# The row maxima of four attention heads: one pair of VectorE reductions instead of two

## What is computed

```
q = rms_norm(linear(layernorm(x), q_w, q_b), norm_q_w)      # 8 x 112 x 512
k_img, k = rms_norm(linear(ctx[:, :257], ...)), rms_norm(linear(ctx[:, 257:], ...))
img_x = softmax(q k_img^T / sqrt(32)) v_img                 # 16 heads
txt_x = softmax(q k^T / sqrt(32)) v
x = x + linear(img_x + txt_x, o_w, o_b)
x = x + sum over the top 2 of 8 experts: weight * W3 gelu(W2 gelu(W1 layernorm(x)))
```

## Time and profile before

| what | value |
|---|---|
| median of 3 executions | 930.0 us (927.8 to 933.55) |
| the profiled execution | 931.23 us |
| its span, first to last instruction | 929.4 us |
| PE busy | 773.7 us (83%) |
| DVE busy | 588.3 us (63%) |
| ACT busy | 505.8 us (54%) |
| instructions on DVE | 1001 |
| mean granted TensorE clock | 0.931 of full speed |
| chain that ended last, by engine | PE 68%, DVE 9%, ACT 9%, issue 7%, DMA 3%, POOL 2% |

### The profile page before, as it was taken

The page is one execution under the profiler, slowest core; times in us unless marked ns, Lnnn a source line. Parts: engine busy times, 40 slices in busy tenths (PEclk is TensorE's granted clock), DMA queues, the critical chain, the costliest instruction groups (busy, mean ns, idle before and its releaser), DMA issues.

```text
span 929.4 us, 17429 instructions
## 1 busy us (share of the span) xinstructions
PE 773.7 (83%) x6238; PEld 676.3 (73%) x6238; DVE 588.3 (63%) x1001; ACT 505.8 (54%) x1154; POOL 69.6 (7%) x94
## 2 busy tenths in 40 slices
PE   2888989898989898773079999999999999999930
PEld 2566666666666666552079999999999999999920
DVE  5466767676767676746136767676767676767634
ACT  4566767676767676751044545454545555555510
POOL 2100000000000000000600000000000000000014
PEclk9989999999999999855579999999999999999975
DMA  7850102010202000407625656565656565656568
GB/s 245 312 210 1 64 11 64 12 64 11 63 12 65 11 22 11 158 11 260 204 86 187 233 184 236 185 235 183 236 184 236 184 236 184 234 183 237 181 226 259
DMA packets 33982, 137.53 MB, mean 148 GB/s; under 512 B 3712, under 2 KB 3728, under 8 KB 22928
## 3 DMA queue, kind: packets, MB, share of 16 engines
q1 hardware_dynamic: 31200, 129.23, 40.0%
q0 software_dynamic: 2736, 7.69, 2.9%
HBM read 115.36 MB, written 21.54 MB: 147 GB/s over the span
## 4 chain that ended last, share of the span: by engine, by line
PE 68%; DVE 9%; ACT 9%; issue 7%; DMA 3%; POOL 2%; SPq 0%; POOLq 0%; ACTq 0%; DVEq 0%
PE tiles L960 7%; PE tiles L962 7%; PE tiles L961 7%; PE scores L1191 4%; PE scores L1193 4%; PE scores L1192 4%; PE ptb L1051 3%; PE pvb L962 3%; PE pvb L961 3%; PE pvb L960 3%; PE ptb L962 3%; PE ptb L961 3%; PE ptb L960 3%; PE scores L1042 2%; ACT scr L543 2%
## 5 line engine op out<-in xcount | busy, mean ns | idle before, releaser
L776 DVE TENSOR_TENSOR w<-scr,w 128x2048 fp32r<-128x2048 f32 x76 | 174.2, 2292 | 84.6 <-ACT w L568 84.6
L568 ACT ACTIVATE w<-scr 128x2048 fp32r<-128x2048 f32 x76 | 144.8, 1907 | 63.2 <-PE scores L1193 59.3
L960 PE MATMUL tiles<-c,w 128*128 128x256 f32 (+1 forms) x272 | 83.0, 305 | 22.1 <-DVE c L672 17.5
L1051 PE MATMUL ptb<-ident,scr 112*128 112x112 f32 x384 | 64.4, 279 | 25.9 <-ACT scr L553 25.9
L960 PE MATMUL tiles<-w 128*128 128x256 f32 x288 | 81.5, 283 | 0.0
L961 PE MATMUL tiles<-w 128*128 128x256 f32 x288 | 81.5, 283 | 0.0
L962 PE MATMUL tiles<-w 128*128 128x256 f32 x288 | 81.5, 283 | 0.0
L961 PE MATMUL tiles<-c,w 128*128 128x256 f32 (+1 forms) x272 | 79.9, 294 | 0.0
L962 PE MATMUL tiles<-c,w 128*128 128x256 f32 (+1 forms) x272 | 79.9, 294 | 0.0
L1051 PEld LDWEIGHTS ptb<-ident,scr 112*128 112x128 f32 x384 | 44.1, 149 | 48.9 <-ACT scr L545 35.1
L553 ACT ACTIVATE scr<-ptb 128x336 f32<-128x336 f32 x128 | 59.9, 468 | 26.9 <-PE ptb L1051 26.9
(11 more groups left out here) (212 smaller groups left out, 2120.9 us busy)
## 6 DMA issues: line engine op xcount, KB each, us to landing
scr<-in_dram SPq DMA_DIRECT2D x86, 1024.0 KB, 4.8
slots_d<-xr SPq DMA_DIRECT2D x3, 2048.0 KB, 17.5
scr<-in_dram SPq DMA_DIRECT2D x8, 750.0 KB, 4.9
scr<-slots_d SPq DMA_DIRECT2D x10, 512.0 KB, 4.6
slots_d<-scr SPq DMA_DIRECT2D x9, 512.0 KB, 3.8
xn<-in_dram SPq DMA_DIRECT2D x10, 256.0 KB, 4.7
xb<-in_dram SPq DMA_DIRECT2D x8, 224.0 KB, 4.9
xr<-in_dram SPq DMA_DIRECT2D x8, 224.0 KB, 2.5
```

The costliest lines, as they stand in the source:

```text
L568: act.activation(EH[slot], raw[slot], ACT.Copy).then_inc(S["eh_done"], 1)
L776: dve.tensor_tensor(EL[slot], raw[slot], EH[slot].bitcast(F32), ALU.subtract).then_inc(S["el_done"], 1)
L960: pe.matmul(out, wh, xh, start=start, stop=False)
L1051: mm = pe.transpose(ptb[:, t * L:(t + 1) * L], probs[0:L, h % 4, t * P:(t + 1) * P], ident[0:L, 0:L])
```

## The change

`maxima` loses its argument i: one call takes all four heads, so its two reductions run over 4 x 257 and 4 x 118 values instead of 2 x 257 and 2 x 118, and there is one call to a group instead of two. `max_done` rises by 1 for each group (4 for each sequence instead of 8), and every head of the group waits for that one. No other instruction is moved on any engine. What is computed stays the same.

```diff
@@ weigh @@
-                act.wait_ge(S["max_done"], (NH * b + h) // 2 + 1)
+                act.wait_ge(S["max_done"], NC * b + h // 4 + 1)
@@ maxima @@
-            def maxima(b, g, i):
+            def maxima(b, g):
 
                 dve.wait_ge(S["s_ready"], NC * b + g + 1)
-                of = nmax[0:L, g % 2, 2 * i:2 * i + 2, :]
-                dve.tensor_reduce(of[:, :, 0], scores[0:L, 2 * i:2 * i + 2, 0:IMG], AX.X, ALU.max, negate=True)
-                dve.tensor_reduce(of[:, :, 1], scores[0:L, 2 * i:2 * i + 2, IMG:KEYS], AX.X, ALU.max, negate=True).then_inc(S["max_done"], 1)
+                of = nmax[0:L, g % 2, :, :]
+                dve.tensor_reduce(of[:, :, 0], scores[0:L, :, 0:IMG], AX.X, ALU.max, negate=True)
+                dve.tensor_reduce(of[:, :, 1], scores[0:L, :, IMG:KEYS], AX.X, ALU.max, negate=True).then_inc(S["max_done"], 1)
@@ body on VectorE @@
                     if h % 4 == 0 and has_heads(b):
-                        maxima(b, h // 4, 0)
-                        maxima(b, h // 4, 1)
+                        maxima(b, h // 4)
```

## The result

The changed kernel is slightly slower: 935.62 us, median of 15 executions (933.64 to 937.43), against 931.86 us, median of 15 of the kernel before (927.80 to 934.77). The ratio is 1.0042 with a 95% interval of 1.0026 to 1.0057, so +3.9 us (2.4 to 5.3). The forecast was +4.8 us, slower by 0.5%, and within 1%. A ratio is taken from the single executions and can differ by 0.0006 from the quotient of the medians. One execution of it in each of these two series, of 1046 and of 4171 us, is left out. The profiled execution took 935.39 us, its span is 933.6 us against 929.4 of before.

The account below looks back on a forecast made before the run. No engine fills the time; the waits count, chiefly ScalarE's first exponentials waiting for L754 in 11 of 32 groups. Terms 1.9 + 0.7 + 2.3 = 4.9 us (4.8 with small covers) on 930.0 gave 934.8 us, range 929.5 to 939.0.

Parts of the forecast that it names:

- The price of a reduction: VectorE's maxima: 1.22 and 0.64 us each, VectorE gaining 0.12 to 0.13 us a group, first exponential possible 0.79 us later.
- Step 12: Sequences 1 to 6: of the exponential's 0.79 us delay, 0.44 us comes through, the rest covered by TensorE's v0.
- Step 0: Sequences 1 to 6: path through VectorE's L672 to TensorE's k0, -0.13 us each; ScalarE's 0.14 us delay fits in idle time.
- Steps 4 and 8: Sequences 1 to 6: exponential already starts behind other ScalarE work, cover 0.6 us, so the change costs nothing.
- Sequence 0: -0.13 us at step 0 through VectorE, nearly all of +0.79 us at step 12: 0.7 us.
- Sequence 7: No projection copies cover the delay: +0.79 us at step 0, +0.79 at step 8, +0.73 at step 12; together 2.3 us.
- The store of x1 in sequence 7: Step 4's +0.79 us is covered: step 8's maxima stand behind L682, waiting for this store behind three weight loads.
- The sum: Whole kernel: 1.9 + 0.7 + 2.3 = 4.9 us slower, or 4.8 with the small covers left in.
- the count of waits: ScalarE's waits for L754: some 18 in place of 11, with new ones of about 0.1 us at step 0 and last step 12.
- (a): Rival: later exponentials hidden, only VectorE's time counts in all 32 groups, -4.2 us, 925.8 us; chance 10%.
- (b): Rival: the delay is exposed at all 32 groups, +25 us, 955 us; chance 7%.
- (c): Rival: longer waits bring TensorE's clock fall a group forward in sequence 7 or make one in sequence 0, 937 to 940 us; 10%.

Follow-up runs that it names:

- the dose of 0.91 us: Against the kernel before: two pairs of reductions kept, but every head of a group waits for both pairs; 937.74 us, ratio 1.0074.

## Why the prediction was right

- **The price of a reduction** (1.22 and 0.64 us from the slope between two sizes): 1.228 and 0.639. VectorE's gain of 0.12 to 0.13 us a group: 1.82 - 1.69 = 0.13 us. The delay of 0.79 us: 1.81 - 1.02 = 0.79.
- **Step 12**, +0.44 each in sequences 1 to 6: +0.46 (12.97 against 12.51), and L1021's idle time 0.45 longer. With two pairs again at step 12 and wide reductions elsewhere, the cost of these sequences was gone.
- **Step 0**, -0.13 each: -0.12 in the changed kernel, -0.12 to -0.13 with two pairs at step 12. That is a small reading; moving L672 by 0.6 us confirmed it with a larger one.
- **Steps 4 and 8**, sequences 1 to 6: nothing, as forecast; step 4 to 8 takes 10.37 to 10.41 us and step 8 to 12 12.60 to 12.65 us in all four profiles of the two kernels.
- **Sequence 0**, forecast +0.7: step 12 to 0 went from 12.96 to 13.67 us, +0.71 where +0.79 was taken as the upper end. Its term at step 0 (-0.13) can't be read, since that stretch varies by more than 1 us. Sequences 0 to 6 together were forecast at 2.6 us and measured 2.2 (1.0 to 3.5).
- **Sequence 7**, forecast +2.3: +1.8 (0.8 to 2.8) with the wide reductions there only. Its three waits have the forecast sizes: step 0 to 4 is 0.70 us longer (0.79), the exponential of step 8 starts 1.82 us after the first reduction instead of 1.03 (+0.79), and that of step 12 3.16 us after the scores instead of 2.42 where the clock is at half in both (+0.74, forecast 0.73).
- **The store of x1 in sequence 7** is the step that isn't confirmed. The forecast let the normalisation L682, which ends the cover of step 4, move by 0.79 us with the three weight loads ahead of the store. The loads do come later, 6.66 us after the scores of step 0 instead of 5.87, but L682 does not follow: 17.72 us after these scores with wide reductions in sequence 7 only, 17.80 and 16.85 in the two profiles before. From the loads to L682 it is 10.9 to 11.1 us in four of the five profiles in which the exponentials of steps 0, 4 and 8 are held back (in the fifth, 11.7 us, VectorE itself came late), and 11.9 to 12.1 us in four of the five without that, 11.0 in the fifth, an unchanged kernel. Where the distance is the shorter one, up to 1 us of the price is given back. Whether the change brings it about is open, and so the agreement of 1.8 with 2.3 us is in part luck. With the store early and the clock at half, the maxima of step 8 stand behind their scores instead: 388.07 + 1.29 = 389.36 us, and they start at 389.41.
- **The sum**: 4.8 forecast, 3.9 (2.4 to 5.3) and 4.9 (3.3 to 6.6) measured. A difference of 1% was said to be what a measurement can tell from none; 15 executions of each kernel told it to 1.5 us, 0.16%.
- **What was off**: the count of waits. 18 were expected and the view of L754 has 12: at step 0 the exponential is 0.15 us late (191.02), but the row shows no idle time ahead of it. The last step 12 was expected to wait 0.1 us and waits 0.94 us in the first profile, 0.63 in the second. And a single pair of profiles would have misled: outside the middle sequences it differs from the forecast by more than the whole effect.
- **The rivals**: (a), only VectorE's time, would have been -4.2 us. Its mechanism is real at step 0 of sequences 1 to 6, 0.12 to 0.13 us each; at steps 4 and 8 of these sequences nothing was gained, and at step 12 the exponential is on the path. The Trainium skill (VectorE: DVE Perf Modes, Rules for kernel authors) says to keep the number of VectorE instructions low; here 64 fewer freed 32 x 0.13 us of VectorE, and the trace shows the time only at step 0 of the middle sequences. As a rule for this kernel's time it gives the wrong sign. (b), exposed everywhere, would have been +25 us; the dose of 0.91 us in all 32 groups cost 6.9 us, not 29. (c), a clock fall brought forward: the sequences 1 to 6 stay at a granted clock of 1.00. In sequence 7 the clock falls 16.4 and 16.6 us after the first scores in the two profiles before, and 19.0 and 13.7 us after them in the changed kernel. In the second of these step 4 to 8 takes 9.48 us instead of 8.31, so a fall one group forward did occur once. Over steps 0 to 12 the changed kernel still has less time at half clock (6.8 and 8.2 us) than the kernel before (11.1 and 9.9), while the kernel that is wide in sequence 7 only has more (13.4), so no price of the change is seen in it. The prediction's reading that TensorE mostly waited ahead of the fall was wrong: it was busy 13.02 of the 16.00 us from 371 to 387.

## What to carry to other kernels

Merging two instructions saved 0.06 us for each one less on the engine that runs them, but the first consumer then waits for the whole: price both ends, and ask at every place of the program which of the two is on the path. The list of who waited for the line, place by place, gave the sum to within its error; the same delay of 0.79 us was worth 0.7, 0.45 or 0 us depending on what stood behind the waiting instruction. Where places differ, the width can be chosen by place: wide at steps 0, 4 and 8 and two pairs at step 12 took 0.6 us off sequences 1 to 6. The same with pairs throughout sequence 7 was not run, and 0.6 us is less than these intervals can tell. Look first at the order on the engine that the path goes through: moving one VectorE instruction ahead of two others gained more (5.5 us) than the change lost.

## What the runs showed of the hardware

- A maximum over four PSUM banks costs by its values alone, 1.05 ns each and about 0.145 us fixed: 393, 639, 685 and 1228 ns for 236, 472, 514 and 1028 values.
- Independent VectorE instructions start 0.08 us before the end of the one ahead (0.60 us after the start of one of 0.68 us; 1.14 after one of 1.22 in the changed kernel).
- TensorE's granted clock in sequence 7 falls to half (1.2 GHz) at different moments in executions of one program (at about 394 us and at about 389 us in the two profiles of the changed kernel), and at times rises to 2.4 GHz for some microseconds between. In these two profiles step 4 to 8 took 8.31 and 9.48 us. In sequence 0 the same twelve products took 2.70 us at a granted clock of 0.50 (kernel before) and 1.52 us at 1.00 (L672 moved).
- The store of x1 behind three weight loads lands at two distances from the loads' issue: the normalisation behind it starts 11.9 or 11.0 us after it in the two profiles of the kernel before. No cause was found.
